# Expert slots: a table in DRAM written by GpSimd scatters in place of one-hot products

## The reference, cut to what matters

```python
CAPACITY_FACTOR = 1.25
C = max(1, math.ceil(CAPACITY_FACTOR * T / E))   # T = 6250, E = 8: C = 977
probs = jax.nn.softmax(x @ gate_w + gate_b, axis=-1)
idx = jnp.argmax(probs, axis=-1)                 # a token's expert
prb = take_along_axis(probs, idx)                # its probability
one_hot = jax.nn.one_hot(idx, E)
pos = (jnp.cumsum(one_hot, axis=0) * one_hot).sum(-1) - 1   # its place in the expert's queue
kept = pos < C
buf = zeros((E, C, D)).at[idx, pos].set(x, mode='drop')
y_tok = ffn_of_each_expert(buf)[idx, min(pos, C - 1)] * (prb * kept)
```

## Time and profile before

| what | value |
|---|---|
| median of 3 runs | 1460.66 us (1456.71 to 1464.74) |
| the profiled execution's own time | 1463.94 us |
| its span | 1462.7 us |
| granted TensorE clock, mean | 0.97 |
| busy: PE, DVE, ACT, POOL | 1305.0, 1198.4, 934.8, 799.2 us |

### The profile page before, as it was taken

One profiled execution on the slowest core, in us unless ns is written; L12 is line 12 of the kernel. 1 busy time (PEld: TensorE's weight loads), 2 busy tenths in 40 slices (PEclk: granted clock), 3 DMA queues, 4 the chain that ended last, 5 costly groups with the idle time before them and its releaser, 6 DMA issues. The chain is left out here.

```text
span 1462.7 us, 38776 instructions
## 1 busy us (share of the span) xinstructions
PE 1305.0 (89%) x14051; PEld 1091.4 (75%) x14053; DVE 1198.4 (82%) x2455; ACT 934.8 (64%) x2122; POOL 799.2 (55%) x629
## 2 busy tenths in 40 slices
PE   4698888995879999998989998999999898989987
PEld 3355555562768888887878887888886687979986
DVE  7797888898869888998899888989984577767786
ACT  4486777776546676665756666657665556565754
POOL 5357445206238888888888884000000577676574
PEclk8799999997989999999999999999999999999999
DMA  9625431002826655666655664121114433343220
GB/s 301 209 57 118 93 77 37 29 23 93 255 64 114 120 99 99 99 99 131 107 105 122 108 101 75 38 73 38 38 38 138 126 118 122 95 136 116 74 79 25
DMA packets 96441, 145.71 MB, mean 100 GB/s; under 512 B 14249, under 2 KB 72262, under 8 KB 96123
## 3 DMA queue, kind: packets, MB, share of 16 engines
q0 software_dynamic: 46080, 69.85, 26.0%
q1 hardware_dynamic: 50186, 73.61, 15.1%
HBM read 105.08 MB, written 60.14 MB: 113 GB/s over the span
## 5 line engine op out<-in xcount | busy, mean ns | idle before, releaser
L1688 PE MATMUL bank<-reg_b,reg_a 128*128 128x256 f16 x4410 | 597.3, 275 | 8.5 <-ACT reg_a L1277 8.0
L1277 ACT ACTIVATE reg_a<-bank 128x392 f16<-128x392 f32 x720 | 343.0, 496 | 214.7 <-PE bank L1680 187.2
L1688 PEld LDWEIGHTS bank<-reg_b,reg_a 128*128 128x128 f16 x4410 | 396.8, 98 | 51.0 <-issue 10.2
L976 POOL DMA_INDIRECT reg_a<-h_rows,reg_d x216 | 395.1, 1829 | 66.2 <-issue 66.2
L1964 DVE TENSOR_TENSOR reg_c<-iota_v,reg_c 128x2048 f16<-128x2048 f16 (+1 forms) x282 | 368.2, 1321 | 45.3 <-ACT reg_c L1170 15.6
L1680 PE MATMUL bank<-reg_a,reg_c 128*128 128x98 f16 x2880 | 243.0, 209 | 16.1 <-ACT reg_a L1277 10.2
L1680 PEld LDWEIGHTS bank<-reg_a,reg_c 128*128 128x128 f16 x2880 | 200.4, 99 | 32.4 <-issue 17.4
L1964 DVE TENSOR_TENSOR reg_a<-iota_h,reg_c 128x1568 f16<-128x1568 f16 x180 | 174.3, 968 | 0.0
L990 POOL COPY take_idx<-inv_i 128x8 int32<-128x8 int32 (+1 forms) x8 | 1.7, 217 | 240.5 <-DVE inv_i L2515 240.5
L1920 PE MATMUL bank<-w_hi,hid_hi 128*128 128x256 f32 (+1 forms) x368 | 107.3, 292 | 12.1 <-DVE w_lo L2550 6.9
L1922 PE MATMUL bank<-w_hi,hid_lo 128*128 128x256 f32 (+1 forms) x368 | 104.6, 284 | 0.0
(11 more groups left out here) (370 smaller groups left out, 2520.6 us busy)
## 6 DMA issues: line engine op xcount, KB each, us to landing
reg_b<-in_L_ffn_w SPq DMA_DIRECT2D x16, 1024.0 KB
h_rows<-reg_b POOLq DMA_DIRECT2D x14, 896.0 KB, 9.8
tok_rows<-reg_e SPq DMA_DIRECT2D x24, 512.0 KB
x_bias<-in_x SPq DMA_DIRECT2D x1, 6250.0 KB
x_bias<-b_out_rows POOLq DMA_DIRECT2D x10, 625.0 KB
x_t<-x_bias SPq DMA_DIRECT2D x24, 256.0 KB
xnT_t<-xnT_rows SPq DMA_DIRECT2D x24, 256.0 KB
out<-reg_e SPq DMA_DIRECT2D x24, 256.0 KB
```

The costliest lines, as they stand in the source:

```text
L976: ins = g.indirect_dma_start(out=acc[i % 2][m][k], out_offset=None, in_=h_rows, in_offset=at, compute_op=ALU.add)
L1277: return a.activation(AT[k].rearrange("p h (w t) -> p h w t", w=2)[:, :, :, s * GROUP:(s + 1) * GROUP], tile_ps[bk][:, 0:GROUP * 2 * NB].r ...
L1688: ins = t_.matmul(agg_ps[k][:, 0:D], AT[k][:, h, :], h_all[:, half, h, :], start=(first and h + half == 0), stop=(last and h == NB - 1 and ...
```

## The change

The token numbers and probabilities no longer go through one-hot products for the first 23 pairs. A table `slot_rows` in DRAM has one row of two f32 (token number, probability) for each of the 8192 slots. It is zeroed early by a DMA from the zeroed `inv_acc`. `route` writes, for each token, the number of its row (`slot_row`) and its probability (`token`), and signals `slot_hot`. POOL then issues two indirect DMAs per pair (`scatter_pair`), each of which writes 128 rows of 8 bytes; rows beyond the table are left out. In `sparse`, these scatters stand between the gathers at places worked out from `GATHER_FROM`, `GATHER_SLOTS` and `SCATTER_LATE`, and those of pairs 15 to 21 behind the last gather; the last one (pair 22) is in POOL's tail. `place` and `add_slots` stay for the last three blocks alone; SP loads the table back into `slot_tab`, and `add_slots` adds the two. Cut to its core:

```diff
+GATHER_FROM = 40
+GATHER_SLOTS = 2.3
+SCATTER_LATE = 24
...
+    slot_rows = dram("slot_rows", (NE * CROWS, 2))
...
+    wq_room = wq[:, :, :].rearrange("p c e -> p (c e)")
+    n = 2 * NE * CT
+    slot_tab = wq_room[:, 0:n].rearrange("p (c w) -> p c w", w=2)
+    token = wq_room[:, n:n + 2 * NB].rearrange("p (b w) -> p b w", w=2)
+    slot_row = wq_room[:, n + 2 * NB:n + 3 * NB].bitcast(I32)
+    n += 3 * NB
+    token_now = wq_room[:, n:n + 4].rearrange("p (m w) -> p m w", w=2)
+    slot_row_now = wq_room[:, n + 4:n + 6].bitcast(I32)
...
-    PLACES = {2: Places(9, 9, 8, 14, 12), 14: Places(9, 9, 8, 16, 16), 10: Places(9, 11, 12, 18, 20),
-              6: Places(9, 9, 8, 14, 12)}
-
     def places_of(q):
-        return PLACES[(KEYS_AT - starts[q]) % SLOTS]
+        return Places(9, 11, 12) if (KEYS_AT - starts[q]) % SLOTS == 10 else Places(9, 9, 8)
...
+        sp.wait_ge(inv_added, 1)
+        sp.dma_start(slot_rows.rearrange("(p c) w -> p (c w)", p=P), inv_acc[:, :]).then_inc(xb_in, 16)
...
         load_w2(0)
         load_b2(0, 0)
+        sp.wait_ge(placed, 16 * 2 * (NQ - 1))
+        sp.dma_start(slot_tab, slot_rows.rearrange("(p c) w -> p c w", p=P)).then_inc(w_in2, 16)
         finished(NQ)
...
-                pool.wait_ge(xb_in, 32)
+                pool.wait_ge(xb_in, 48)
...
+        def scatter(q, tokens_, rows_):
+            for m in range(2):
+                g.indirect_dma_start(out=slot_rows, out_offset=bass.IndirectOffsetOnAxis(ap=rows_[:, m:m + 1], axis=0),
+                                     in_=tokens_[:, m, :], in_offset=None, bounds_check=NE * CROWS - 1, oob_is_err=False
+                                     ).then_inc(placed, 16)
+
+        def scatter_pair(q):
+            pool.wait_ge(slot_hot, q + 1)
+            scatter(q, token[:, 2 * q:2 * q + 2, :], slot_row[:, 2 * q:2 * q + 2])
...
         def tail():
             more(NB - 1, rounds_of(pool, NB - 1))
+            scatter_pair(NQ - 2)
...
                 for j in range(GROUNDS):
                     for m in range(2):
+                        at_slot = GATHER_FROM + GATHER_SLOTS * ((i * GROUNDS + j) * 2 + m)
+                        while scattered + 1 < q and at_slot >= starts[scattered + 1] + SCATTER_LATE:
+                            scatter_pair(scattered)
+                            scattered += 1
                         k = j % GACC
...
+            for q in range(scattered, NQ - 2):
+                scatter_pair(q)
...
-                pe.wait_ge(inv_added, q)
...
-            first(NQ - 1, 14)
...
-                            pe.wait_ge(inv_added, placed + 1)
-                            if counted:
-                                pe.wait_ge(slot_hot, counted)
+                        if place_ < 0 and counted:
+                            pe.wait_ge(slot_hot, counted)
...
-                        if q and at == of.place:
-                            place(q - 1)
-                            placed += 1
...
+            if (b, c) == (2, 2):
+                v_.tensor_copy(token[:, :, 0], node_1[:, :])
...
-        def add_slots(p):
-            dve.wait_ge(inv_added, p + 1)
-            dve.wait_ge(slot_used, p + 2)
-            v_.tensor_tensor(inv_acc[:, :], inv_acc[:, :], inv_ps, ALU.add).then_inc(inv_added, 1)
+        def add_slots():
+            dve.wait_ge(w_in2, 96)
+            dve.wait_ge(slot_used, 2)
+            halves_ = inv_acc[:, :].rearrange("p (w c) -> p w c", w=2)
+            v_.tensor_tensor(halves_, slot_tab.rearrange("p c w -> p w c"),
+                             inv_ps.rearrange("p (w c) -> p w c", w=2), ALU.add).then_inc(inv_added, 1)
 
         def route(p, q, w=2, o=pair_route):
             pos, drop, base, place, slot = o.pos, o.drop, o.base, o.place, o.slot
+            prb = o.prb if w == 3 else token[:, ds(p * 2, 2), 1]
...
+            if w == 2:
+                step(v_.tensor_tensor(slot, base, pos, ALU.add), q)
+                v_.tensor_scalar(o.low_i, slot, P - 1, None, ALU.bitwise_and)
+                step(v_.tensor_scalar(o.high_i, slot, 7, None, ALU.arith_shift_right), q)
+                step(v_.scalar_tensor_tensor(o.low_i, o.low_i, float(NE * CT), o.high_i, ALU.mult, ALU.add), q)
+                v_.tensor_tensor(slot_row[:, ds(p * 2, 2)], o.low_i, drop, ALU.add).then_inc(slot_hot, 1)
+                return
...
-            dve.wait_ge(slot_used, p + 1)
...
-                        if at == places_of(q).add and q:
-                            add_slots(q - 1)
...
-        dve.wait_ge(inv_added, NQ + 1)
+        dve.wait_ge(inv_added, 2)
```

More of the change, by code:

```diff
@@ L95 @@
 KSTEP = 256.0
-ROUTE_STEPS = 11
+ROUTE_STEPS = 10
 MIX_STEPS = 6
@@ L439, in build @@
         sem(n) for n in ("route_d", "route_exp", "route_hot", "route_cum", "slot_hot", "slot_used", "inv_added"))
+    placed, slot_copied = sem("placed"), sem("slot_copied")
     inv_set, inv_dve = sem("inv_set"), sem("inv_dve")
@@ L462, in build @@
         r_log, r_diff, r_eq, r_exp, r_cum, r_hot, r_top, r_first, r_sum, r_prb, r_pos, r_drop, r_base, r_place,
-        r_slot, r_low_i, r_high_i, hots[:, 0:2 * P].rearrange("p (m v) -> p m v", m=2),
-        hots[:, 4 * P:5 * P].rearrange("p (m v) -> p m v", m=2), hots[:, 2 * P:4 * P].rearrange("p (m v) -> p m v", m=2),
-        gate_ps, cum_ps)
+        r_slot, r_low_i, r_high_i, None, None, None, gate_ps, cum_ps)
     places = iter(range(ATN, 2 * ATN))
@@ L512, in build @@
     gs_of = [g_s if q in (0, NQ - 2, NQ - 1) or q % 2 == 0 else g_alt for q in range(NQ)]
-    Places = namedtuple("Places", "mix count route place add")
+    Places = namedtuple("Places", "mix count route")
     KEYS_AT = 2
-    PLACES = {2: Places(9, 9, 8, 14, 12), 14: Places(9, 9, 8, 16, 16), 10: Places(9, 11, 12, 18, 20),
-              6: Places(9, 9, 8, 14, 12)}
     def places_of(q):
-        return PLACES[(KEYS_AT - starts[q]) % SLOTS]
+        return Places(9, 11, 12) if (KEYS_AT - starts[q]) % SLOTS == 10 else Places(9, 9, 8)
     def active(p, s):
@@ L942, in gnn, with second @@
                 more(b - 1, rounds_of(pool, b - 1))
+            fin(0)
+        def scatter(q, tokens_, rows_):
[6 more added lines that the diff above has]
+            scatter(q, token[:, 2 * q:2 * q + 2, :], slot_row[:, 2 * q:2 * q + 2])
+        def second(q, s):
+            if first_pair(q):
+                return
+            pool.wait_ge(slot_hot, q)
+            apart(pool)
+            if not fixed(q, 1):
+                pool.wait_ge(placed, q * 32 - 32)
+                apart(pool)
+            g.tensor_copy(token_now, token[:, ds(q * 2 - 2, 2), :])
+            g.tensor_copy(slot_row_now, slot_row[:, ds(q * 2 - 2, 2)]).then_inc(slot_copied, 1)
+            pool.wait_ge(slot_copied, q)
+            apart(pool)
+            scatter(q, token_now, slot_row_now)
         def tail():
             more(NB - 1, rounds_of(pool, NB - 1))
+            scatter_pair(NQ - 2)
         def sparse():
@@ L962, in sparse @@
             landed = [[[0] * GACC for m in range(2)] for _ in range(2)]
+            scattered = 0
             for i, q in enumerate(GATHERED):
@@ L979, in sparse @@
                         landed[i % 2][m][k] += 1
-        main_phase(pool, gnn, lambda b, s: None, lambda q, s: None, lambda q, s: None, tail, sparse)
+            for q in range(scattered, NQ - 2):
+                scatter_pair(q)
+        main_phase(pool, gnn, lambda b, s: None, lambda q, s: None, second, tail, sparse)
         pool.wait_ge(agg_done, NB)
@@ L1754, in first @@
                 ins.then_inc(fin_mix, 1)
-            if s == 14 and not first_pair(q):
-                place(q - 1)
         def second(q, s):
             w, o = blocks_of(q), fin_of(q)
-            if s == -1:
-                pe.wait_ge(inv_added, q + 1)
+            if s == -1 and not first_pair(q):
+                pe.wait_ge(slot_hot, q)
             if s == 10:
@@ L1828, in tail @@
             busy(12)
-            pe.wait_ge(inv_added, NQ)
             place(NQ - 1, 3, last_route)
@@ L1843, in sparse @@
             pe.sem_inc(agg_done, GB)
-            counted, placed = 0, 0
+            counted = 0
             for p in range(3, len(DENSE)):
@@ L1856, in sparse @@
                         of = places_of(q)
-                        if q and at in (of.count, of.place):
+                        if q and at == of.count:
                             pe.wait_ge(key_out, min(b + (2 if s >= KEYS_AT else 1), NB))
-                        if q and at == of.count:
                             count(q - 1)
@@ L2331, in first @@
             if c == 3:
-                if not first_pair(q) and not fixed(q, NQ) and not sums:
-                    add_slots(q - 1)
                 if not fixed(q, NQ):
@@ L2404, in choose @@
             ins.then_inc(route_hot, 1)
-        def add_slots(p):
-            dve.wait_ge(inv_added, p + 1)
-            dve.wait_ge(slot_used, p + 2)
-            v_.tensor_tensor(inv_acc[:, :], inv_acc[:, :], inv_ps, ALU.add).then_inc(inv_added, 1)
```

(7 more changed lines are left out.)

4 lines of the change are left out of this document (1 added, 3 removed).

## The result

The changed kernel takes 1492.84 us (median of 4 runs, 1484.53 to 1497.31), the kernel before 1461.97 on the same chip (1456.71 to 1464.74): ratio 1.021, 95% interval 1.015 to 1.026, or +30.9 us. It is slower; whether by more than 2% the interval leaves open. The forecast was 1487.5 within 1474 to 1504. The profiled execution took 1497.31 us, its span is 1496.1.

The account below looks back on a forecast made before the run. PE's work and POOL's list bound the phase, POOL's slightly longer. Second landing +38.0 us, less PE's 9.5 behind it, gives +28.5; less 1.5 in the tail, +27 on the median 1460.66: 1487.5 us, range 1474 to 1504.

Parts of the forecast that it names:

- POOL's list ends the phase, not PE's work: Edge-summing phase up to 903 us: POOL's issue list is longer than PE's work by a few microseconds.
- Price of a scatter: On POOL: 1.24 us plus a gap of 0.30, 1.54 us each, bounds 1.25 and 2.0.
- Where they stand: Scatters among the gathers: 12 before pair 8's last gather, 18 more before pair 16's, the other 16 after.
- The stalls and landings: DVE idles about 23 us at pair 8, landing 683.7, and 37 us at pair 16, landing 941.5.
- the give-back of the second stretch: POOL's gathers up to pair 16: quicker while DVE idles for 37 us, giving back 5.0 us.
- PE's gain before the landing is swallowed, behind it kept: Edge-summing phase: gains before pair 16's landing vanish in the wait; PE's 9.5 us behind it stays.
- The tail: After the phase: 1.5 us gained (bounds 0 and 3.2), the table's load hidden with 5 us to spare.
- The sum: Whole kernel: +28.5 us at the phase's end, less 1.5 in the tail, +27 us in total.
- dearer scatters: Rival, POOL: scatters at 2.0 us, or 0.46 us of waiting for slot_hot each: 1499 us, chance 0.13.
- no give-back: Rival, POOL's gathers: no faster while DVE idles, +8 us, 1496 us, chance 0.10.
- No net change: Rival, POOL: scatters at 0.6 us with the gap, for their small rows: 1461 us, chance 0.06.
- a small packet would keep nearly the price of a gather's: DMA engines: overhead per descriptor dominates, 0.132 us a packet, 1.06 us per 128, still hidden behind POOL's issue.

Follow-up runs that it names:

- e2: The changed kernel with each of the 30 scatters among the gathers issued twice, the second time into a table nobody reads: 1536.23 us, ratio 1.053.
- e4: The kernel before, with 30 POOL operations of 128x384 f32 where the changed kernel has its scatters among the gathers: 1498.30 us, ratio 1.027.
- e1: The changed kernel with the 30 scatters that stood among the gathers issued behind the last gather: 1477.18 us, ratio 1.012.
- run 704: Not a label of a run: 704 counts the packets in e1's run of scatters behind the last gather; e1 took 1477.18 us.
- e9: The changed kernel with pairs 10 and 19 gathered, plus 30 scatters to an unread table in one run behind the last gather: 1466.73 us.
- e11: As e9, but 30 plain gathers of 1 KB rows in place of the 30 extra scatters: 1467.10 us, ratio 1.001.

## Why the prediction was right

- *POOL's list ends the phase, not PE's work*: shown by e2 and e4, where only that list grew.
- *Price of a scatter*: 1.24 + 0.30 forecast; from 480 to 943 us it is 1.26 + 0.30:

```profile
L958 POOL DMA_INDIRECT slot_rows<-reg_w x30 | 37.9, 1262 | 9.1 <-issue 9.1
```

- *Where they stand*: 12 before pair 8's last gather, 30 in all, as counted from the code.
- *The stalls and landings*: 23 us forecast, 24.0 + 1.6 measured, landing 683.7 and 684.0. Second: 37 forecast, 40.5 + 1.4 measured, landing 941.5 and 945.3. That the first fits to 0.3 us is luck: the gathers began 2.4 us later (427.7 for 425.4), and POOL's list up to pair 8's last gather grew by 16.4 us for 15.3, but the landing came 3.2 us behind the end of that gather (680.8) and not 6.4 as before (662.0 and 668.4). The sum had no term for the late start nor for the quicker landing. At the second landing the last gather ended at 942.2 for a forecast 935.9, and 3.0 us to land in place of 5.6 took part of that back.
- *The step that was mis-sized* is the give-back of the second stretch, which lasted 261.3 us for 257.8. I had the gathers win 5.0 us while DVE idles, and counted nothing for them elsewhere. Pair 16's gathers, before and after:

```profile
L976 POOL DMA_INDIRECT reg_a<-h_rows,reg_d x108 | 196.4, 1818 | 33.3 <-issue 33.3
...
L1018 POOL DMA_INDIRECT reg_a<-h_rows,reg_d x108 | 194.3, 1799 | 33.4 <-issue 32.6 <-DMA reg_a<-h_rows,reg_d 0.8
```

  The 19 in DVE's idle time gave back 19 x 0.27 = 5.1 us, but the 90 from 684 to 906 (one lies across the cut and counts in both) took 1.849 and not 1.818, 2.8 us more. Net 2.3 us, 2.7 short of the forecast. The scatters took 27.9 for 27.7, and 0.6 us more lies in how the two landings followed their gathers: 3.5 us. Why a gather beside DVE was dearer than before is open.
- *PE's gain before the landing is swallowed, behind it kept*: the last gathered addition moved by 945.3 − 903.4 = 41.8 us, the end of PE's last block sum by 1151.4 − 1119.3 = 32.1. Kept: 9.7, forecast 9.5.
- *The tail*: the last slot products moved by 1166.4 − 1136.4 = 30.0, a gain of 2.1 for 1.5. The table's load is hidden: SP issued it at 1157.4, PE's last products wait for DVE's one-hots, 1.66 us, and the addition that needs the table waits for these products:

```profile
1157.41 0.43 SPq L764 DMA_DIRECT2D reg_w<-slot_rows  x1
...
1166.38 0.94 PE L1836 MATMUL bank<-reg_c 128*128 128x128 f32 x6 [1.66 <-DVE reg_c L2484]
...
1167.43 0.29 DVE L2443 TENSOR_TENSOR inv_acc<-reg_w,bank 128x128 f32<-128x128 f32 x1 [1.10 <-PE bank L1836]
```

- *The sum*: +30.0 at that point for a forecast +27.0. The expert stage behind it is 3.4 us longer in the profiled execution; the change touches nothing there, and the medians differ by 30.9.

Of the rivals, "dearer scatters" and "no give-back" end near the measured time as well (1499, 1496), but neither happened as told: a scatter cost 1.57 us and not 2.0, and the gathers took 1.55 us wherever DVE idled. In sum they lost 5.0 us over both stretches, where the forecast had 8.2 and the second rival 0. "No net change" would have needed scatters of 0.6 us.

I was also wrong, without harm, that a small packet would keep nearly the price of a gather's. In e1's run 704 packets took 2.0% of 16 engines for 28 us, 0.013 us each against 0.13, and 21 scatters made them, some 33 each and not 128. I had drawn it from the Trainium skill (DMA: Bandwidth & Descriptors, Why small descriptors are slow) without doing its sum: it gives some 3 cycles fixed for a packet beside one per 32 bytes, by my estimate 35 cycles for a 1 KB row and 4 for 8 bytes. The trace agrees with that ninefold fall: it shows a tenfold one.

## What to carry to other kernels

Before moving work to the engine with the lowest busy share, look at what else is in its instruction order and who needs the last of it: an engine at 55% of the span can be the bound of a stretch in which it has no gap but its own issue. Count the price of a small DMA by its issue on the engine, not by its bytes. When an addition to such a stream costs more than it saves, move the consumer later before undoing the change (here 37 us better than before by one constant), and do not pack what was taken out into one run elsewhere.

## What the runs showed of the hardware

- An indirect DMA of 128 rows costs GpSimd 0.95 to 1.0 us and a gap of 0.30 when DVE is idle, for 8-byte rows written, 8-byte rows read and 1 KB rows read alike (e9 to e11); the accumulating form takes 1.55. Beside DVE at work the 8-byte writes took 1.31 and the accumulating form 1.85.
- Some thirty such DMAs in a row, 1.25 to 1.30 us apart, bring PE, DVE and ACT nearly to a stop from some 10 to 16 us into the run up to 3 us behind it, and cost 40 to 43 us here. At one per 3.5 us the trace has some 9 us in the same place. Why, and why the accumulating gathers do not do it, stays open.
